# Layer 1's experts: rows loaded in 512-byte pieces by four tiles and turned by VectorE's block transpose

## The reference, cut to what matters

```python
x = hidden_states.reshape(-1, H)                    # T = 2048 tokens, H = 512
...                                                 # scores, group mask
_, top_k_index = jax.lax.top_k(masked, K)           # K = 8 of E = 32 experts
flat_idx = top_k_index.reshape(-1)
sort_idx = jnp.argsort(flat_idx)
xs = jnp.repeat(x, K, axis=0)[sort_idx]             # 16384 rows, by expert
gate = jax.lax.ragged_dot(xs, w_gate, group_sizes)  # H x 256 per expert
up = jax.lax.ragged_dot(xs, w_up, group_sizes)
down = jax.lax.ragged_dot(jax.nn.silu(gate) * up, w_down, group_sizes)
routed = (down[unsort].reshape(T, K, H) * tkw[..., None]).sum(axis=1)
return (routed + shared).reshape(hidden_states.shape)
```

## Time and profile before

| | us |
|---|---|
| median of three runs (3,118.14 to 3,126.93) | 3,120.46 |
| the profiled execution's own time | 3,133.18 |
| its span, from first to last instruction | 3,131.5 |
| TensorE busy, of the span | 2,768.3 (88%) |
| VectorE busy | 1,433.1 (46%) |
| GpSimd busy | 1,366.4 (44%) |
| ScalarE busy | 773.1 (25%) |

### The profile page before, as it was taken

One profiled execution on the slowest core, in us unless ns is written; L12 is line 12 of the kernel. 1 busy time (PEld: TensorE's weight loads), 2 busy tenths in 40 slices (PEclk: granted clock), 3 DMA queues, 4 the chain that ended last, 5 costly groups with the idle time before them and its releaser, 6 DMA issues. The chain is left out here.

```text
span 3131.5 us, 34748 instructions
## 1 busy us (share of the span) xinstructions
PE 2768.3 (88%) x9569; PEld 1263.4 (40%) x9572; DVE 1433.1 (46%) x2766; ACT 773.1 (25%) x1190; POOL 1366.4 (44%) x960
## 2 busy tenths in 40 slices
PE   5887975799999887689999998972999999999997
PEld 2343431344444333233333334431555555555453
DVE  7999999332001232266665647211333333333332
ACT  4746653200000010134334332000111111111111
POOL 2777656133000131136646331465455555455554
PEclk8999999999999998889999998996999999999999
DMA  4333222310300699750474001555766666777654
GB/s 124 114 101 106 76 67 54 112 55 14 113 0 14 231 343 326 207 149 1 128 197 111 1 1 64 213 202 179 159 136 151 150 112 130 191 152 151 132 90 72
DMA packets 303703, 386.00 MB, mean 123 GB/s; under 512 B 51058, under 2 KB 208307, under 8 KB 303602
## 3 DMA queue, kind: packets, MB, share of 16 engines
q1 hardware_dynamic: 212434, 243.23, 25.0%
q0 software_dynamic: 68272, 97.19, 16.1%
q10 hardware_dynamic: 22896, 44.30, 5.2%
HBM read 237.10 MB, written 160.27 MB: 127 GB/s over the span
## 5 line engine op out<-in xcount | busy, mean ns | idle before, releaser
L1859 POOL DMA_INDIRECT out_x<-e_yo,e_dest x318 | 493.1, 1551 | 465.3 <-DMA out_x<-e_yo,e_dest 289.6
L1994 PE MATMUL e_psg<-e_wgu,e_xsT 128*128 x1272 | 580.3, 599 | 3.1 <-SPq L1830 1.9
L285 POOL TENSOR_TENSOR hc<-hs,bcst 128x1024 f32<-128x1024 f32 x128 | 300.7, 2349 | 179.6 <-DVE ps_b L505 171.3
L1994 PEld LDWEIGHTS e_psg<-e_wgu,e_xsT 128*128 128x128 f32 x1272 | 228.9, 190 | 235.7 <-issue 234.1
L630 PE MATMUL ps_y<-hc,ident 128*128 128x512 f32 x512 | 241.0, 609 | 88.0 <-POOL hc L285 87.8
L2010 PE MATMUL e_pso<-e_wd,e_hT 128*128 x636 | 298.9, 592 | 0.7 <-DVE e_hT L1935 0.7
L1940 DVE TENSOR_TENSOR e_h<-e_psg,e_sg 128x256 f32<-128x256 f32 x159 | 67.5, 425 | 502.1 <-ACT e_sg L1880 502.1
L511 DVE TENSOR_TENSOR_SCAN hs<-dA,ps_b 128x1024 f32<-128x1024 f32 x128 | 292.7, 2286 | 7.5 <-ACT dA L415 3.3
L1233 PE MATMUL r_ps_t<-r_wd,r_h 128*128 128x512 f32 x480 | 211.2, 601 | 8.7 <-DVE r_h L982 5.1
L1880 ACT ACTIVATE e_sg<-e_psg 128x256 f32<-128x256 f32 x159 | 60.9, 383 | 638.8 <-PE e_psg L1994 638.8
L415 ACT ACTIVATE dA<-dt,a_neg 128x511 f32<-128x511 f32 x256 | 165.1, 713 | 101.9 <-DVE hs L511 96.8
(11 more groups left out here) (414 smaller groups left out, 3795.8 us busy)
## 6 DMA issues: line engine op xcount, KB each, us to landing
e_xs<-slots_in ACTq DMA_DIRECT2D x159, 272.0 KB, 3.1
slots_in<-zeros SPq DMA_DIRECT2D x160, 256.0 KB, 2.3
bcst<-bc_rows SPq DMA_DIRECT2D x128, 256.0 KB, 4.3
e_wgu<-in_wg SPq DMA_DIRECT2D x32, 512.0 KB, 5.2
e_wgu<-in_wu SPq DMA_DIRECT2D x32, 512.0 KB, 6.2
e_wd<-in_wd SPq DMA_DIRECT2D x32, 512.0 KB, 7.1
e_w<-in_wg SPq DMA_DIRECT2D x11, 1408.0 KB, 16.1
e_w<-in_wu SPq DMA_DIRECT2D x11, 1408.0 KB, 18.1
```

The lines of the kernel that those rows point to most:

```text
L285: pool.tensor_tensor(hc[:, it % 2, half(h), :], hs[:, it % 2, half(h), :], bc(bcst[:, q, 1, :], 1, HB), ALU.mult).then_inc(sem["hc"], 1)
L1859: pool.indirect_dma_start(halves, bass.IndirectOffsetOnAxis(dest[:, q, a:a + 1], 0), yo[:, q, a * HC:(a + 1) * HC], None, bounds_check=2 * ...
L1994: j = pe.matmul(ps_g[:, q % 2, :], xsT[:, q % 2, k, :], wgu[:, bass.ds(e % RING, 1), k, :], start=k == 0, stop=k == KH - 1)
```

## The change

Rows and records are loaded apart. Of four tiles' rows, 512 x 512 values, one load takes 128 columns into 32 partitions: partition a * 32 + j gets, of each of 16 blocks of 32 rows, row j's columns from a * 128 on, as a piece of 512 bytes. Four such loads make a group; there are two buffers for groups. VectorE turns a tile's part, 16 blocks of 32 x 32 for each quarter of the partitions, in one block transpose from SBUF to SBUF, which gives the same `e_xsT` as before. TensorE's row transposes, their PSUM buffer and the semaphore `tr` go. The records of four tiles come in a fifth load, 17 words per row. TensorE reads the expert's number before the hidden values' transposes. A minimum of one row per expert is added to the count that gives an expert's tiles, in the routing. The diff, cut:

```diff
-                    step(dve.tensor_scalar(tf[:, :], ps_r[:, 0:E], float(P - 1), None, ALU.add))
+                    step(dve.tensor_scalar(tf[:, :], ps_r[:, 0:E], 1.0, float(P - 1), ALU.max, ALU.add))
...
-        xs = pl.sb("e1_xs", [P, RING, XW])
+        DQ = 32
+        NQ = P // DQ
+        RECW = 2 * K1 + 1
+        xs = pl.sb("e1_xs", [P, 2, RING * NQ, P])
+        rec = pl.sb("e1_rec", [P, 2, RING, XW - H])
...
-                def load(t, q):
-                    act.dma_start(xs[:, q % RING, :], D["xs1"][bass.ds(t * P, P), :]).then_inc(rows_in[q % RING], 16)
+                def load_rows(row0, r):
+                    for a in range(NQ):
+                        act.dma_start(xs[a * DQ:(a + 1) * DQ, r, :, :],
+                                      D["xs1"][bass.ds(row0, RING * P), a * P:(a + 1) * P].rearrange("(s j) c -> j s c", j=DQ))\
+                           .then_inc(rows_in[r], 16)
+
+                def load_rec(row0, r):
+                    act.dma_start(rec[:, r, :, 0:RECW], D["xs1"][bass.ds(row0, RING * P), H:H + RECW]
+                                  .rearrange("(u p) w -> p u w", p=P)).then_inc(rec_in[r], 16)
 
                 def reload(t, q):
-                    hold(act, sem["tr"], 1 + t + 1, c["held"])
-                    hold(act, sem["dest"], 1 + t + 1, c["held"])
-                    load(t + RING, q)
+                    if q % RING == RING - 2:
+                        hold(act, sem["xsT"], 1 + t + 2, c["held"])
+                        load_rows((t + RING + 2) * P, q // RING)
+                    if q % RING == 1:
+                        hold(act, sem["dest"], 1 + t - 1, c["held"])
+                        load_rec((t + RING - 1) * P, 1 - q // RING)
...
-                def turned_rows(t, q):
-                    dve.wait_ge(sem["tr"], 1 + t + 1)
-                    dve.wait_ge(sem["gu"], 1 + t - 1)
-                    dve.tensor_copy(xsT[:, q % 2, :, :], ps_x[:, q % 2, :].rearrange("p (k s) -> p k s", s=P))\
-                       .then_inc(sem["xsT"], 1)
+                def turned_rows(t, q, n, first=False):
+                    if q % RING == 0:
+                        dve.wait_ge(rows_in[q // RING % 2], 16 * NQ * n)
+                    if not first:
+                        dve.wait_ge(sem["gu"], 1 + t - 1)
+                    part = slice(q % RING * NQ, (q % RING + 1) * NQ)
+                    dve.transpose(xsT[:, q % 2, :, :].rearrange("p k (s j) -> p k s j", j=DQ),
+                                  xs[:, q // RING % 2, part, :].rearrange("p s (i k) -> p k s i", k=KH)).then_inc(sem["xsT"], 1)
...
-                def turn_rows(q, landed_count):
-                    pe.wait_ge(rows_in[q % RING], landed_count)
-                    for k in range(KH):
-                        j = pe.transpose(ps_x[:, q % 2, k * P:(k + 1) * P], xs[:, q % RING, k:H:KH], c["ident"][:, :])
-                    j.then_inc(sem["tr"], 1)
...
                         t = i * RING + q
-                        if not (last and q == LAST - 1):
-                            pe.wait_ge(sem["xsT"], 1 + t)
-                            turn_rows(q + 1, 16 * (i + 1 + (q + 1) // RING))
+                        e = expert_of(t)
                         if not (first and q == 0):
                             turn_hidden(t - 1, q + RING - 1)
-                        up(t, q)
+                        up(t, q, e)
```

More of the change, by code:

```diff
@@ L1808, in expert_stage1 @@
         ps_o = pl.ps("e1_pso", [P, 2, 512])
-        sem = {n: pl.sem("e1_" + n) for n in ("ids", "w0", "w1", "w2", "w3", "ready", "tr", "xsT", "gu", "sg", "h",
+        sem = {n: pl.sem("e1_" + n) for n in ("ids", "w0", "w1", "w2", "w3", "ready", "xsT", "gu", "sg", "h",
                                               "htr", "hT", "down", "yo", "added", "preset", "iota", "named", "chosen", "first", "dest")}
         landed = [sem[f"w{s}"] for s in range(RING)]
-        rows_in = [pl.sem0(f"e1_rows{q}") for q in range(RING)]
+        rows_in = [pl.sem0(f"e1_rows{r}") for r in range(2)]
+        rec_in = [pl.sem0(f"e1_rec{r}") for r in range(2)]
         half_out = [pl.sem0(f"e1_out{a}") for a in range(2)]
@@ L1888, in empty @@
                        .then_inc(sem["yo"], 1)
-                def load(t, q):
-                    act.dma_start(xs[:, q % RING, :], D["xs1"][bass.ds(t * P, P), :]).then_inc(rows_in[q % RING], 16)
-                def reload(t, q):
-                    hold(act, sem["tr"], 1 + t + 1, c["held"])
-                    hold(act, sem["dest"], 1 + t + 1, c["held"])
-                    load(t + RING, q)
-                for q in range(RING):
-                    load(q, q)
+                def load_rows(row0, r):
[6 more added lines that the diff above has]
+                                  .rearrange("(u p) w -> p u w", p=P)).then_inc(rec_in[r], 16)
+                def reload(t, q):
+                    if q % RING == RING - 2:
[4 more added lines that the diff above has]
+                        load_rec((t + RING - 1) * P, 1 - q // RING)
+                for r in range(2):
+                    load_rows(r * RING * P, r)
+                    load_rec(r * RING * P, r)
                 for t in range(OUT):
                     gate(t, t)
+                    if t > 1:
+                        reload(t, t)
                     if t > 0:
-                        reload(t - 1, t - 1)
                         empty(t - 1, t - 1, first=True)
                 gate(OUT, 0)
-                reload(OUT - 1, OUT - 1)
                 empty(OUT - 1, OUT - 1, first=True)
@@ L1919, in _ @@
                     gate(t, q)
[L1920 to L1921 removed]
+                    if q == 1:
+                        reload(t, q)
                     empty(t - 1, q + OUT - 1)
@@ L1940, in product, with addressed @@
                     dve.tensor_tensor(h[:, q % 2, :], ps_g[:, q % 2, F1:], sg[:, q % 2, :], ALU.mult).then_inc(sem["h"], 1)
-                def addressed(t, q):
-                    row = xs[:, q % RING, :]
+                def addressed(t, q, n):
+                    row = rec[:, q // RING, q % RING, :]
+                    if q % RING == 0:
+                        dve.wait_ge(rec_in[q // RING], 16 * n)
                     if not (isinstance(t, int) and t < OUT):
@@ L1952, in addressed @@
                     dve.tensor_reduce(wrow[:, q, :], mine[:, q % 2, :], AX_X, ALU.add).then_inc(sem["chosen"], 1)
-                    dve.scalar_tensor_tensor(out=dest[:, q, 0:1], in0=pad[:, q % 2, :], scalar=-1.0, in1=row[:, H + 2 * K1:H + 2 * K1 + 1],
+                    dve.scalar_tensor_tensor(out=dest[:, q, 0:1], in0=pad[:, q % 2, :], scalar=-1.0, in1=row[:, 2 * K1:RECW],
                                              op0=ALU.add, op1=ALU.add).then_inc(sem["first"], 1)
                     dve.wait_ge(sem["first"], 1 + t + 1)
-                    dve.tensor_tensor(dest[:, q, 1:2], pad[:, q % 2, :], row[:, H + 2 * K1:H + 2 * K1 + 1], ALU.add)\
+                    dve.tensor_tensor(dest[:, q, 1:2], pad[:, q % 2, :], row[:, 2 * K1:RECW], ALU.add)\
                        .then_inc(sem["dest"], 1)
@@ L1966, in a_round @@
                         product(t, q)
-                        addressed(t, q)
+                        addressed(t, q, i + 1)
                 dve.wait_ge(sem["iota"], 1 + 2)
@@ L1972, in _ @@
                 dve.wait_ge(sem["preset"], 1 + 2)
-                dve.wait_ge(sem["tr"], 1 + 1)
-                dve.tensor_copy(xsT[:, 0, :, :], ps_x[:, 0, :].rearrange("p (k s) -> p k s", s=P)).then_inc(sem["xsT"], 1)
+                turned_rows(0, 0, 1, first=True)
                 a_round(0, first=True)
```

22 lines of the change are left out of this document (11 added, 11 removed).

## The result

| | before | after |
|---|---|---|
| median (7 runs each) | 3,122.47 us | 3,108.30 us (3,106.22 to 3,112.24) |
| ratio, 95% interval | | 0.995 (0.9939 to 0.9961) |
| profiled execution: own time, span | 3,133.18, 3,131.5 | 3,106.26, 3,104.5 |
| first stretch, tile 0's scatter to tile 131's | 779.7 | 773.7 |
| last 27 tiles, tile 131's to tile 158's | 157.2 | 139.9 |

The kernel got faster by 0.5%, 14.2 us; the forecast was 13.2 us slower. The measured time lies inside the range, the sign is wrong.

A forecast was written before the change was run, and what follows sets the result against it. GpSimd's chain of adding scatters was to replace TensorE as the bound: +27.2 us in the first stretch, -17.1 in the last 27 tiles, +3.1 at the start, together +13.2 on 3120.5, so 3,133.7 us; range 3,064 to 3,178 us.

The forecast's parts named there:

- The bound: Last stage: TensorE binds now; without row transposes its tile takes 5.40 us and GpSimd's chain of adding scatters binds instead.
- The undisturbed period: GpSimd's scatters: from one tile's first half to the next with no load beside it, 4.61 us.
- The burst: Four row loads issued at once every fourth tile: delay the scatters' chain 2.92 us, plus 0.2 for the small load.
- The refill: Loading one expert's weights: delays the scatters' chain 3.45 us, 29 times in the first stretch, 100.1 us in all.
- the crossing: Price of a burst of row loads below which the kernel gets faster instead of slower: 2.57 us.
- The length of a burst: Engine time of four bunched row loads: 4.05 us, from 1.01 us per zero fill in 512-byte pieces.
- Last 27 tiles: End of the stage, without refills: the scatters' chain sets the pace, 140.1 us instead of 157.2, so -17.1 us.
- The start: First product of the stage waits for four row loads instead of one: +3.1 us.
- the rival of a wait on TensorE's path by VectorE: VectorE or the read of the expert's number makes TensorE wait 0.46 us a tile: 3,151 us, chance 3%.
- The expert's number "at nothing": TensorE's read, moved ahead of the hidden tile's transposes, stands behind four down matmuls of 0.43 us each: costed at nothing.
- The faster rival: Bunched row loads do little to the scatters and TensorE stays the bound: 3,051 to 3,061 us, chance 32%.
- The longer burst: Rival: row loads writing only 32 partitions take longer than their bytes say, as long as a refill: 3,154 us, chance 20%.

## Why the prediction was wrong

- **The bound: right.** The scatters' chain takes TensorE's place, and TensorE, let free, runs 5.39 us a tile (forecast 5.40).
- **The undisturbed period: right.** 4.60 us in the last ten periods (forecast 4.61).
- **The burst: the step that failed.** "If a burst delays the chain as a refill does, in proportion, it costs 3.45 x 4.05 / 4.78 = 2.92 us per four tiles." The first stretch leaves at most 2.50 us for a burst with its small load, against 2.92 + 0.2, and a second burst adds 2.06, though its engine time is 4.7 us and not 4.05; in proportion it would be 3.45 x 4.7 / 4.78 = 3.4. The proportion doesn't carry over from one kind of load to another: a refill costs the chain at least 63% of its engine time (3.03 of 4.78), a burst with its small load at most 49% (2.50 of 5.1). Nor is a burst's price one number, with 3.9 us in the last tiles. Why a burst costs less for its length than a refill stays open.
- **The refill: too dear.** At least 3.03 us for 3.45, from three periods, and 28 of them instead of 29. Of the 807.0 - 773.7 = 33.3 us that the first stretch is shorter than forecast, the bursts and small loads make 103.0 - 84.9 = 18.1 and the refills 100.1 - 84.9 = 15.2; with refills at 3.45 it would be 29.8 and 3.5. By either split the bursts' part alone turns the sign of +13.2. The prediction had put the crossing at 2.57 us a burst, and the price fell on the other side of it. Two errors inside the step pull against each other, a refill too dear and a burst too short: with the refill mended alone, 3.03 x 4.05 / 4.78 = 2.57 would have come near the 2.50, by luck.
- **The length of a burst: too short.** 1.01 us a load came from zero fills of 256 KB in 512-byte pieces, in a window with 20 fills of 16 KB as well; the row loads measured 4.7 / 4 = 1.2.
- **Last 27 tiles: right in the sum, by luck in part,** 139.9 us against 140.1. There are four bursts and not five, and they cost 3.9 us with their small loads instead of 3.12.
- **The start: right in sign, half the size,** 5.7 us for 3.1. The first block transpose had to wait for four loads issued with four more and a small one behind them, and the wait from issue to first use grew by 5.1 us.
- **TensorE's busy share: 96% in the first stretch, not 91%.** It does more than 131 tiles there: 1,090 records of the gate and up product at eight a tile are 136, since it ends the stretch with a lead over the scatters that it didn't have at the start.
- **VectorE: right.** 1.10 us where 0.7 was taken, and hidden; the rival of a wait on TensorE's path by VectorE didn't come.
- **The expert's number "at nothing": right as an edit in this change, wrong as a reading of the kernel before.** The read was not fully covered there, 599 ns against 592 in the page's groups. Moved alone it is worth 15 us by the medians, 9.5 by the stretches.
- **The faster rival** gave 3,051 to 3,061 us; it had the sign for a reason that isn't so. Bursts do cost, and TensorE isn't the bound. The longer burst (3,154) had the length right and the price wrong.

With the measured parts in place of the forecast's the sum is 3,133.7 - 33.3 (first stretch) - 0.2 (last 27 tiles) + 2.6 (start) = 3,102.8 us, which is 3,120.5 - 17.7. The measured 3,108.3 lies 5.5 above: 2.0 because seven runs put the median of before at 3,122.5, and 3.5 between the profiles' stage and the medians.

## What to carry to other kernels

When a chain of dependent DMAs is the next bound, price everything that shares the engines with it by taking it out and by doubling it, not by its bytes or its engine time: each of the four loads of a burst cost 0.2 us less when it went out alone, and a second burst cost 2.06 us on average in one stretch and 0.9 in another. Count in the trace how many loads an edit really removes before dividing by them. Don't bunch loads beside such a chain; the spreading was worth 33 us here and the change itself 14. And take a change apart before crediting it: of two parts, one was worth the whole and the other nothing, while on a TensorE without the chain the two together take its tile from 5.9 to 5.39 us, over 70 us in all, and either alone leaves it at 5.86 to 5.90.

## What the runs showed that was not expected

- A value read by TensorE's queue costs 0.4 to 0.5 us a tile behind two transposes of 0.12 us, and some nanoseconds a matmul behind six. The profile books the second kind as busy time: compare the mean of one instruction between two lines that do the same.
- Four loads to 32 partitions in 512-byte pieces, with their small load, hold the engines 5.1 us where the same bytes as 2,048-byte rows to 128 take 3.8, and the scatters pay 0.3 us of it.
- After 79.9 us of idle time TensorE's first eight matmuls take 6.5 us and the next eight 3.6, with the granted clock at 0.50 in the first 4 us. The low clock at the stage's end, 0.92 on average, falls behind TensorE's last product and costs nothing.
